# The head of a fused attention and expert layer: a first projection from whole float32, multiplications by zeros, and another order on three engines

## The reference

```python
# attention: 16 query heads of 128, 4 key and value heads, each shared by 4 query heads
q, k, v = x @ Wq, x @ Wk, x @ Wv
qs, ks = softmax(q), softmax(k)              # over the 128 features of a head
gl = log_sigmoid(k) / 16                     # the gate's logarithm
sq, sk = rotary(q), rotary(k)
# gated linear attention: S = S * exp(gl) + ks * v ; o_gla = qs @ S, token by token
# softmax attention:      y = softmax(causal(sq @ sk / sqrt(128))) @ v
x = layernorm(x + (0.5 * y + 0.5 * o_gla) @ Wo)
# experts: softmax over 8 router logits, the best 2 of each token
x = layernorm(x + sum over the 2 experts of weight * (silu(x @ Wg) * (x @ Wu)) @ Wd)
```

## Time and profile before

| | |
|---|---|
| median of 3 runs | 990.01 us (987.09 to 993.39) |
| profiled execution | 990.93 us |
| its span, first to last instruction | 989.0 us |
| mean granted clock of TensorE | 0.979 |
| TensorE busy | 924.6 us, 93% of the span |
| VectorE, ScalarE, GpSimd busy | 643.2, 661.8, 620.6 us |

### The profile page before, as it was taken

The page is one execution under the profiler, slowest core; times in us unless marked ns, Lnnn a source line. Parts: engine busy times, 40 slices in busy tenths (PEclk is TensorE's granted clock), DMA queues, the critical chain, the costliest instruction groups (busy, mean ns, idle before and its releaser), DMA issues.

```text
span 989.0 us, 18166 instructions
## 1 busy us (share of the span) xinstructions
PE 924.6 (93%) x5332; PEld 720.6 (73%) x5332; DVE 643.2 (65%) x1483; ACT 661.8 (67%) x2139; POOL 620.6 (63%) x612
## 2 busy tenths in 40 slices
PE   3899999999999999999999999999999989999870
PEld 2767787878777777878778787877777766777650
DVE  4676767676767676767676969676887664321164
ACT  4777777777777777777777777776667664455442
POOL 6658775767565657677767667776658880230374
PEclk9899999999999999999999999999999999999995
DMA  7101100000000000700000000010102121343444
GB/s 247 33 17 33 39 1 1 6 12 6 1 0 0 0 0 7 256 7 1 1 2 1 1 7 6 1 62 2 62 1 78 38 84 42 96 134 102 139 139 148
DMA packets 35648, 44.88 MB, mean 45 GB/s; under 512 B 3568, under 2 KB 29552, under 8 KB 35440
## 3 DMA queue, kind: packets, MB, share of 16 engines
q1 hardware_dynamic: 32496, 35.50, 11.3%
q0 software_dynamic: 3072, 8.39, 2.7%
HBM read 25.52 MB, written 18.35 MB: 44 GB/s over the span
## 4 chain that ended last, share of the span: by engine, by line
PE 84%; ACT 5%; DVE 5%; issue 3%; POOL 1%; another core or an unknown queue 1%; DMA 0%; POOLq 0%; DVEq 0%; ACTq 0%; SPq 0%
PE OA L560 13%; PE PR L461 13%; PE S L513 11%; PE MS L533 9%; PE S L542 7%; PE OA L522 5%; PE S L659 5%; PE OA L676 4%; PE OA L553 4%; PE PR L489 3%; PE PR L485 3%; ACT eqk L788 2%; PE MS L474 1%; PE S L504 1%; PE MS L564 1%
## 5 line engine op out<-in xcount | busy, mean ns | idle before, releaser
L1439 POOL TENSOR_TENSOR qd<-eqk,eg 128x512 f32<-128x512 f32 x63 | 74.8, 1187 | 165.4 <-issue 156.5
L560 PE MATMUL OA<-wT,V 128*128 128x512 f32 x320 | 148.4, 594 | 0.0
L750 ACT ACTIVATE S<-S,nm 128x128 f32<-128x128 f32 (+3 forms) x256 | 126.8, 495 | 25.8 <-DVE nm L965 22.5
L788 ACT ACTIVATE eqk<-qkv,nmx 128x128 f32<-128x128 f32 x320 | 124.3, 396 | 6.9 <-DVE nmx L1040 6.4
L965 DVE TENSOR_REDUCE nm<-S 128x2 f32<-128x256 f32 (+3 forms) x128 | 102.0, 817 | 28.0 <-PE S L513 24.8
L1427 POOL TENSOR_TENSOR eqk<-eqk,rse 128x640 f32<-128x640 f32 x63 | 79.9, 1267 | 52.7 <-DVE rse L1083 28.0
L560 PEld LDWEIGHTS OA<-wT,V 128*128 128x128 f32 x320 | 59.5, 190 | 69.4 <-issue 68.9
L999 DVE TENSOR_TENSOR pr<-S,rl 128x256 f32<-128x256 f32 (+3 forms) x128 | 105.5, 825 | 5.3 <-DVE rl L995 0.3
L1416 POOL TENSOR_TENSOR rp<-qkv,cos 128x640 f32<-128x640 f32 x64 | 99.5, 1554 | 7.2 <-ACT qkv L778 7.0
L1419 POOL TENSOR_TENSOR rp<-rp,rt 128x640 f32<-128x640 f32 x64 | 99.5, 1554 | 5.0
L1416 POOL TENSOR_TENSOR rt<-qkv,sin 128x640 f32<-128x640 f32 x64 | 99.1, 1548 | 0.0
(11 more groups left out here) (164 smaller groups left out, 2495.9 us busy)
## 6 DMA issues: line engine op xcount, KB each, us to landing
qkv<-slot_x SPq DMA_DIRECT2D x46, 128.0 KB
slot_y<-eqk SPq DMA_DIRECT2D x46, 128.0 KB
gu_w<-in_wgu SPq DMA_DIRECT2D x8, 352.0 KB, 3.6
slot_x<-zero SPq DMA_DIRECT2D x2, 1280.0 KB, 7.3
stage<-in_wqkv SPq DMA_DIRECT2D x6, 384.0 KB, 3.3
xraw<-in_x_cols SPq DMA_DIRECT2D x16, 128.0 KB, 2.3
acc<-in_x_rows SPq DMA_DIRECT2D x1, 2048.0 KB, 11.5
dn_w<-in_wdn SPq DMA_DIRECT2D x8, 256.0 KB, 4.2
```

The costliest lines, as they stand in the source:

```text
L560: last = pe.matmul(OA[:, :], V[:, j, :], wT[:, j, :], start=(c == 0 and j == 0), stop=(j == c))
L750: nc.scalar.activation(S[:, h, 0:n], S[:, h, 0:n], ACT.Exp, bias=nm[:, h:h + 1], scale=1.0, accum_out=ls[:, h:h + 1]).then_inc(s_exp, 1)
L788: last = nc.scalar.activation(eqk[:, par, h * 128:(h + 1) * 128], qkv[:, c % C, h * 128:(h + 1) * 128], ACT.Exp, bias=nmx[:, h:h + 1], sca ...
```

## The change

TensorE. A new function `keep_warm(n)` issues n multiplications of a tile of zeros, read as bfloat16, with 512 columns, into the PSUM tile `OA`, which nothing reads before it is written anew. It is called with 11 ahead of the first projection, with 4 between the gate sums and the turn of chunk 0, and with 4 inside that turn. A new function `project_whole` makes the projection of chunk 0 of group 0 from `xraw` and `prf`, whole float32, in four multiplications as each half of the weights arrives. The halves `w_hi` and `w_lo` are still made, for the chunks from 1 on.

ScalarE. `gate_logs` of chunk 0 stands ahead of `features`, and `features` of chunk 1 ahead of `q_out` of chunk 0.

VectorE. It does the memsets that GpSimd did, ahead of everything else; `gate_out` of chunk 0 stands ahead of `feature_sums`; the wait for the constants stands behind the decay.

GpSimd. Ahead of `rotate(0, 0)` it splits chunks 0 and 1 of x only. Between `rotate(0, 0)` and the rest it waits for VectorE's decay of chunk 0 (`s_qd`).

SyncE. It waits for the first projection behind the transfer of Wo, ahead of two chunks of x, the weight jobs and `acc`.

```diff
--- before.py
+++ after.py
@@ -373,6 +373,7 @@
             sp.dma_start(cm[:, :], cmat).then_inc(s_cst, 16)
             sp.dma_start(maskb[:, :, :], cmask).then_inc(s_cst, 16)
             sp.dma_start(wTf, wo_in[:, 0:2048]).then_inc(s_wor, 16)
+            sp.wait_ge(s_proj, 1)
             load_x(0, 2)
             load_x(0, 3)
             load_job(0)
@@ -462,6 +463,22 @@
                                          start=(i == 0), stop=(i == len(steps) - 1))
                 last.then_inc(s_proj, 1)
 
+            still = zero[:, 0:HID].bitcast(BF16)
+
+            def keep_warm(n):
+                for _ in range(n):
+                    pe.matmul(OA[:, :], still[:, 0:P128], still[:, :], start=True, stop=True)
+
+            def project_whole():
+
+                pe.wait_ge(s_xr[0], 16)
+                for k in range(KT2):
+                    pe.wait_ge(s_w0[k], 16)
+                    for a, b in ((0, 512), (512, QKV)):
+                        last = pe.matmul(PR[:, a:b], xraw[:, 0, k, :], prf[:, k * QKV + a:k * QKV + b],
+                                         start=(k == 0), stop=(k == KT2 - 1))
+                last.then_inc(s_proj, 1)
+
             def gate_sums(g, c):
 
                 u = C * g + c
@@ -474,7 +491,7 @@
                 pe.matmul(MS[:, 0:128], gmat, gl[:, :], start=True, stop=True)
                 pe.matmul(MS[:, 128:130], gl[:, :], halves, start=True, stop=True).then_inc(s_g, 1)
 
-            def turn(g, c, has_next):
+            def turn(g, c, has_next, between=None):
 
                 u = C * g + c
                 par = c % 2
@@ -484,6 +501,8 @@
                 for h in range(GQ):
                     last = pe.transpose(PR[:, h * 128:(h + 1) * 128], rp[:, par, h * 128:(h + 1) * 128], ident)
                 last.then_inc(s_trq, 1)
+                if between:
+                    between()
                 pe.wait_ge(s_qd, 2 * (u + 1))
                 for h in range(GQ):
                     last = pe.transpose(PR[:, 512 + h * 128:512 + (h + 1) * 128], qd[:, par, h * 128:(h + 1) * 128], ident)
@@ -677,12 +696,15 @@
                                      expert_cols(dn_w, expert[q], k * HID, (k + 1) * HID), start=(k == 0), stop=(k == 1))
                 last.then_inc(s_dn, 1)
 
-            pe.wait_ge(s_splo, 1)
-            project(0, 0, lambda: pe.wait_ge(s_splo, 2))
+            pe.wait_ge(s_tab, 1)
+            keep_warm(11)
+            project_whole()
+            pe.wait_ge(s_splo, 2)
+            project(0, 1)
             pe.wait_ge(s_cst, 64)
-            project(0, 1)
             gate_sums(0, 0)
-            turn(0, 0, True)
+            keep_warm(4)
+            turn(0, 0, True, lambda: keep_warm(4))
             for c in range(C):
                 if c == 1:
                     pe.wait_ge(s_splo, 3)
@@ -898,12 +920,12 @@
                 act.wait_ge(s_w0[i], 16)
                 nc.scalar.copy(w_hi[:, i * QKV:(i + 1) * QKV], prf[:, i * QKV:(i + 1) * QKV]).then_inc(s_sphi, 1)
             copy_out(0, 0)
+            gate_logs(0, 0)
             features(0, 0)
-            gate_logs(0, 0)
             copy_out(0, 1)
             exp_gates(0, 0)
+            features(0, 1)
             q_out(0, 0)
-            features(0, 1)
             qd_out(0, 0)
             gate_logs(0, 1)
             act.wait_ge(s_wor, 16)
@@ -1327,17 +1349,24 @@
                 nc.vector.scalar_tensor_tensor(out=nmr[:, i], in0=mv[2][:, i, 0], scalar=-1.0, in1=rstd[2][:, i],
                                                op0=ALU.mult, op1=ALU.mult).then_inc(s_nmr, 1)
 
+            nc.vector.memset(zero[:, :], 0.0).then_inc(s_tab, 1)
+            nc.vector.memset(neghalf[:, :], -0.5)
+            for e in range(E):
+                if e:
+                    nc.vector.memset(tri8[:, e, 0:e], 1.0)
+                nc.vector.memset(tri8[:, e, e:E], 0.0)
+            nc.vector.memset(ones[:, :], 1.0).then_inc(s_tab, 1)
             for i in range(KT2):
                 dve.wait_ge(s_sphi, i + 1)
                 a = slice(i * QKV, (i + 1) * QKV)
                 nc.vector.tensor_tensor(w_lo[:, a], prf[:, a], w_hi[:, a].bitcast(F32), ALU.subtract).then_inc(s_splo, 1)
-            dve.wait_ge(s_cst, 64)
             prepare(0, 0)
+            gate_out(0, 0)
             feature_sums(0, 0)
-            gate_out(0, 0)
             clamp_gates(0, 0)
             prepare(0, 1)
             decay(0, 0)
+            dve.wait_ge(s_cst, 64)
             k_out(0, 0)
             feature_sums(0, 1)
             gate_out(0, 1)
@@ -1524,22 +1553,18 @@
                 pool.wait_ge(s_ve[2], 2 * n + h + 1)
                 nc.gpsimd.tensor_tensor(rstd[2][:, i], ve[2][:, i], neghalf[:, i], ALU.pow).then_inc(s_rs[2], 1)
 
-            for c in range(3):
+            for c in range(2):
                 x_wait(0, c)
                 x_split(0, c)
-            nc.gpsimd.memset(neghalf[:, :], -0.5).then_inc(s_tab, 1)
-            for e in range(E):
-                if e:
-                    nc.gpsimd.memset(tri8[:, e, 0:e], 1.0)
-                last = nc.gpsimd.memset(tri8[:, e, e:E], 0.0)
-            nc.gpsimd.memset(ones[:, :], 1.0)
-            last = nc.gpsimd.memset(zero[:, :], 0.0)
-            last.then_inc(s_tab, 1)
             pool.wait_ge(s_cst, 64)
             rotate(0, 0)
+            pool.wait_ge(s_qd, 2)
+            x_wait(0, 2)
+            x_split(0, 2)
             rotate(0, 1)
             x_wait(0, 3)
             x_split(0, 3)
+            pool.wait_ge(s_tab, 2)
             for c in range(C):
                 step(0, c, first=True)
             for g in range(1, HEAD):
```

## The result

| | before | changed | 
|---|---|---|
| median | 990.0 us (16 runs) | 982.25 us (16 runs, 978.54 to 985.43) |
| ratio | | 0.9921, 95% interval 0.9904 to 0.9937 |
| profiled execution, its span | 990.93, 989.0 | 978.54, 976.7 |

The change gains 0.8%, 7.8 us (6.2 to 9.5 by the interval). The two spans differ by 12.3 us, more than the medians: the profiled execution of the changed kernel is the fastest of its 16.

The account below looks back on a forecast made before the run. TensorE's long queue bounds the kernel, so the head's shift counts: GpSimd's rotation of chunk 2 at 26.0 instead of 35.94, one difference with overlapping parts not added. 990.93 - 9.9 = 981.0 us, range 977 to 986.5.

Parts of the forecast that it names:

- the rival of the falling clock: TensorE, sparse work from 13 to 20 us: clock falls, chunk 2's projection ends 2.2 to 3.2 us later; 982.4 us, chance 0.25.
- three signs that the prediction named for being wrong: Head: decays over 2 us; wait over 2 us for acc; shift at chunk 2's rotation not the shift at the end.
- The frame: Behind the head, one long TensorE queue: a head edit gains what it brings forward the first steady steps, 9.9 us.
- The projection: TensorE, chunk 0: the zeros raise the clock, projection ends at 8.9 us, ScalarE's copy starts at 8.95 instead of 11.15.
- the clock does not rise for zeros: TensorE's head: projection ends at 11.0, gain 6.6 us, 984.3 us; chance 0.11 together with a third of the gain absorbed.
- The collision: VectorE's five decays of chunk 0 cost what GpSimd's instructions cost; with GpSimd still they end at 15.65 instead of 25.14.
- (c): GpSimd's order: its row behind the decays starts the rotation of chunk 2 at 26.0 instead of 35.94, 9.9 us earlier.
- (d): What else in the head could be later than 26.0: chunk 2's projection hidden at the full clock, acc costing 0 to 0.5 us.
- The first score maximum: VectorE: ready at 20.2 behind chunk 1's gate operation, then waiting for acc to land at 21.5 to 22.0.
- GpSimd being the bound of this stretch: GpSimd, from the decays to the rotation of chunk 2 at 26.0: its idle stretches of 2.9, 3.0 and 2.0 us are gone.
- The held queue: SyncE holds acc behind the first projection: slower once acc lands after 32 us, 993 if the projection ends at 20; chance 0.02.

Follow-up runs that it names:

- e3: Changed kernel with VectorE's wait for acc moved from ahead of its first step to the first addition to acc: ratio 0.9933.
- e5: Changed kernel without GpSimd's wait for the decays, rotating chunks 0 and 1 in a row so that the collision returns: ratio 0.9960.
- e7: Changed kernel with acc's wait late, chunk 1 decayed on VectorE, Wo's low half behind the first score maxima, GpSimd's split of chunk 3 behind the rotation: ratio 0.9916.
- e10: The kernel of e7 again, beside e9 on one chip: ratio 0.9905 to the kernel before, median 971.53 us.
- e2: Changed kernel without any of the 19 multiplications by zeros: ratio 0.9942.
- e1: Kernel before with GpSimd's order alone: split of chunk 2 and rotation of chunk 1 only behind VectorE's decay of chunk 0: ratio 0.9964.
- e9: Changed kernel again, unaltered, with a second profile: ratio 0.9925 to the kernel before, median 973.38 us.
- e11: Changed kernel with only the eleven zeros ahead of the first projection, without the 4 and 4 round the turn: ratio 0.9933.
- e4: The kernel of e3 with VectorE also weighing and decaying chunk 1 and GpSimd waiting for it ahead of rotating chunk 2: ratio 0.9920.

## Why the prediction was right, and where its sum was off

The forecast was 981.0 us with a range of 977 to 986.5; it is 982.25. Part of that closeness is luck. The forecast gain of 9.9 us was taken off the profiled execution, 990.93, which is 0.9 us above the median; off the median it gives 980.1. The measured gain is 7.8 us, and 9.9 lies outside its interval of 6.2 to 9.5. The time is also nearest to the 982.4 of the rival of the falling clock, whose rotation at 26.8 to 27.8 contains the measured 27.43, but it came about in another way, as told below.

Of the three signs that the prediction named for being wrong, one came: a wait of 3.75 us for acc, where over 2 was the line. The decays stayed under 2 us (1.80, of which 0.6 is the end of the rotation of chunk 0), and the shift at chunk 2's rotation, 8.51 us, is 8.35 at the mark and 8.34 at the 57th addition. TensorE is busy for 750.06 of the 760 us that correspond to the old 750.03. Point by point:

- **The frame held.** What the head gains passes through the steps: 8.35 us at the second, 8.34 at the 57th, 7.8 in the medians.
- **The projection.** Copy at 8.46 in the first profile and 8.97 in the second, 8.95 forecast. The zeros do raise the clock: in the changed kernel, e3, e5, e7 and e10 it rose while nothing else had run. One bound was added up wrongly: zeros to 5.9 and 2.6 at the full level end at 8.5, not 8.1. The rival "the clock does not rise for zeros" would have cost less than the 3.3 us I gave it: without any zeros (e2) the mark came 0.7 to 1.2 us later and the ratio tells 1.7 to 2.1 us, with intervals that overlap, since the projection raised the clock for chunk 1 by itself.
- **The collision.** Decays end at 15.46, forecast 15.65. e1 and e5 show that the long durations come from GpSimd's instructions beside them: 1.39 us without, 5.66 with them. GpSimd was through with the move of V at 24.09, forecast 24.4.
- **The term that was off is (c)'s last one with (d):** the decay of chunk 1, forecast from 24.4 to 26.0, ran from 24.97 to 27.43. Of the 1.4 us, 0.57 is the late start. I had put acc's landing at 21.5 to 22.0 with 0 to 0.5 us of cost; it landed at 22.1. The other 0.86 is a collision that I had not looked for: VectorE's low half of Wo against the second instruction of GpSimd's decay, 1.44 us instead of 0.46, less 0.12 by which the sum to 26.0 was rounded up. In e9, where acc landed at 21.6, GpSimd has no idle time there and only the collision is left: the decay started at 24.46, the rotation at 26.90. In step 0 of the old trace the two did not meet, but in a later step they did, and the trace could have told me. VectorE and GpSimd of the kernel before:

```profile
52.06 2.27 DVE L1054 TENSOR_TENSOR wo_lo<-wT,wo_hi 128x1024 fp32r<-128x1024 f32 x1
```

```profile
53.20 1.28 POOL L1448 COPY V<-qkv 128x128 f32<-128x128 f32 x1
```

  The move of V, 0.28 us in the earlier trace rows, took 1.28 there. e1 shows the collision at the same instruction as the changed kernel, e3 at the move of V.
- **The first score maximum was ready earlier than forecast.** I had VectorE's gate operation of chunk 1 wait until 20.1 for the end of a rotation and the maximum ready at 20.2. The gate operation ran at 17.82 for 0.59 us, held only to the end of GpSimd's instruction at 18.27, and without acc the maximum starts at 18.58 (e3). So the wait for acc was 3.75 us and not the 1.3 to 1.8 that the forecast implied.
- **The rival of the falling clock** came true in its mechanism and not in its place or price: the clock fell at 24 to 26 us, in the hole ahead of 24.96, behind chunk 2's projection instead of ahead of it. It was almost wholly hidden: GpSimd's row has no idle time over 0.1 us from 27.43 to the end of chunk 2's decay at 39.0, TensorE's turn of chunk 2 follows at 39.17, and from the rotation of chunk 2 to the mark only 0.16 us of the shift is lost (8.51 to 8.35), although TensorE was at the low level until about 31.6. In e11, without the eight zeros round the turn, it fell at about 17 us, ahead of chunk 2's projection as the rival had it, and the mark was still 52.47. e10, where the clock does not fall and VectorE's row is shorter, is 1.9 us faster; how much of that is the clock alone was not separated.
- **"GpSimd being the bound of this stretch"** was half right. In the first profile GpSimd idles 0.88 us for the chain behind acc, in e9 it does not idle. e4 took 2.8 us out of its row and won nothing at the mark over e3; VectorE's row was just behind. As I read it, three rows stood within a microsecond or two, and an edit of one alone could not show a gain.
- **The held queue** did little harm: acc was issued 0.45 us later and landed at 22.1, inside the stated 20.2 to 23, and what that cost is the 0.57 us above or less. The 9 us in that paragraph do not follow from its own figures (3.1 MB at 2.9 MB in 11.5 us are 12.3 us).

## What to carry to other kernels

In this pipeline an edit of the start was worth the shift that it gave to one mark behind it, and that mark can be followed through the whole trace. Two profiles of one kernel put it 0.2 and 0.5 us apart, where the intervals of the ratios could not tell 1.9 us. But all shifts against the kernel before rested on a single profile of it, and came out 0.4 to 3.7 us larger than the ratios: the common reference should be profiled more than once. Edits of a head need not be additive: at the mark the order of GpSimd was worth 5.2 us alone and 1.85 as the last of the set, in part because a transfer's landing lay between; the ratios are too wide to show it. And when two engines collide, look at every pair of long instructions on both rows in the new timing, since taking one collision out moves the others.
